# Row places in a GNN kernel: running counts per block in PSUM, and block additions spread over VectorE's step

## What is computed

```python
h = jnp.maximum(_layernorm(x), 0.0)
# layer 0: mean over neighbours, two products, log_softmax
x = x + _L0_gnn_ref(h, edge_index, W_l, W_r, b)
h = jnp.maximum(_layernorm(x), 0.0)
# layer 1
weight = jnp.maximum(edge_rbf @ W1 + b1, 0.0) @ W2 + b2   # edge_rbf: 206250 x 64
hl = h @ Wl + bl
msg = hl[dst] * weight
x = x + segment_sum(msg, src)      # the sum goes by src, the unsorted side
```

## Time and profile before

| | |
|---|---|
| median of 3 runs | 3465.89 us |
| span of the profiled execution | 3469.3 us |
| busy share of the span | PE 86%, weight loads 70%, DVE 79%, ACT 60%, POOL 52% |
| instructions that DVE ran | 7718 |
| chain that ended last, by engine | DVE 36%, PE 32%, issue 17%, DVEq 7%, DMA 4% |

### The profile page before, as it was taken

How to read it: one execution, slowest core, us unless ns; L and a number is a source line. 1 busy time by engine, 2 the same in 40 slices (tenths; PEclk the granted TensorE clock), 3 DMA queues, 4 the chain that set the end, 5 groups by cost and what they waited for, 6 DMA issues and landing times.

```text
span 3469.3 us, 97235 instructions
## 1 busy us (share of the span) xinstructions
PE 2987.6 (86%) x26330; PEld 2437.6 (70%) x26331; DVE 2757.6 (79%) x7718; ACT 2085.3 (60%) x4907; POOL 1808.5 (52%) x1790
## 2 busy tenths in 40 slices
PE   0799999999668878899999989988889898998977
PEld 0699999999655556776766666766667666766766
DVE  8899999999786657777777777777777777777866
ACT  2599999998353335555555545555455555555656
POOL 3400010000127777667766676666766677677750
PEclk9999999999868889999999999999999999999999
DMA  3198888960103336666666656655666666666657
GB/s 117 37 326 313 311 309 310 311 213 3 38 19 107 103 103 172 179 175 160 178 164 161 160 150 172 166 162 147 166 168 180 165 158 184 173 158 175 181 154 207
DMA packets 506188, 593.04 MB, mean 171 GB/s; under 512 B 71050, under 2 KB 477058, under 8 KB 505905
## 3 DMA queue, kind: packets, MB, share of 16 engines
q1 hardware_dynamic: 449506, 470.49, 49.4%
q0 software_dynamic: 56400, 119.07, 9.9%
HBM read 293.94 MB, written 295.35 MB: 170 GB/s over the span
## 4 chain that ended last, share of the span: by engine, by line
DVE 36%; PE 32%; issue 17%; DVEq 7%; DMA 4%; POOL 2%; ACT 1%; SPq 0%; POOLq 0%; ACTq 0%
PE PS L1119 11%; DVE X L1017 8%; PE PS L1110 5%; DVE big L990 4%; PE PS L1282 4%; PE PS L1249 4%; DMA messages<-big,idxr 4%; DVE big L978 3%; DVE aux L768 3%; DVEq L1012 3%; DVE big L964 2%; DVE big L975 2%; DVE big L967 2%; DVE hpar L1006 2%; PE PS L1261 2%
## 5 line engine op out<-in xcount | busy, mean ns | idle before, releaser
L605 POOL DMA_INDIRECT messages<-big,idxr x1664 | 1637.0, 984 | 720.8 <-issue 466.5
L1282 PE MATMUL PS<-big,hpar 128*128 128x128 f32 x5120 | 663.8, 283 | 163.7 <-DVE hpar L1006 128.7
L1282 PEld LDWEIGHTS PS<-big,hpar 128*128 128x128 f32 x5120 | 610.5, 195 | 223.1 <-DVE hpar L1006 181.2
L1432 ACT ACTIVATE big<-PS,b1c 128x512 f32<-128x512 f32 x416 | 286.0, 688 | 708.3 <-PE PS L1238 708.3
L1017 DVE TENSOR_TENSOR X<-X,PS 128x128 f32 x1280 | 368.7, 288 | 325.3 <-PE PS L1282 131.9
L1119 PE MATMUL PS<-h_parts,counts 128*128 128x258 f32 x3626 | 565.3, 296 | 0.0
L1359 ACT ACTIVATE counts<-PS 128x784 fp32r<-128x784 f32 x592 | 481.7, 825 | 93.9 <-PE PS L1110 85.6
L1249 PE MATMUL PS<-W2s,big 128*128 128x128 f32 x3328 | 500.8, 295 | 0.0
L1249 PEld LDWEIGHTS PS<-W2s,big 128*128 128x128 f32 x3328 | 419.0, 197 | 98.3 <-issue 98.3
L1119 PEld LDWEIGHTS PS<-h_parts,counts 128*128 128x128 f32 x3626 | 470.2, 191 | 0.2 <-ACT counts L1359 0.2
L1443 ACT ACTIVATE big<-PS 128x512 f32<-128x512 f32 x416 | 247.6, 595 | 347.2 <-PE PS L1261 339.4
(11 more groups left out here) (222 smaller groups left out, 3639.1 us busy)
## 6 DMA issues: line engine op xcount, KB each, us to landing
messages<-zeros SPq DMA_DIRECT2D x896, 193.5 KB
big<-messages SPq DMA_DIRECT2D x320, 516.0 KB
aux<-slot_rows SPq DMA_DIRECT2D x416, 128.0 KB
big<-in_edge_attr_dram SPq DMA_DIRECT2D x402, 128.0 KB
messages<-big,idxr POOLq DMA_INDIRECT x1664
X<-in_x_dram SPq DMA_DIRECT2D x12, 448.0 KB, 6.9
out_dram<-X SPq DMA_DIRECT2D x6, 448.0 KB
edge_places<-big SPq DMA_DIRECT2D x1, 2496.0 KB, 13.2
```

What stands on the lines that cost most here:

```text
L605: pool.indirect_dma_start(strm_d, bass.IndirectOffsetOnAxis(ap=idxr[:, n % U, j:j + 1], axis=0), outr[:, n % U, j, :], None).then_inc(S_sc ...
L1282: last = nc.tensor.matmul(to[:, r * C:(r + 1) * C], finhot[:, n % 2, r * 2 + q, :], fin[:, k, r, q * ROW:q * ROW + C], start=(q == 0), sto ...
```

## The change

The counts of `taken` move into PSUM. A part's first `ranks` writes the starts of its blocks into `pQ` by a product with the identity, and every later one adds to `pQ` what has passed since: the rows of the step before (in a ring `hotW` of RING = 8 steps) and those of the step's own earlier tiles. `pQ` then holds each place outright. VectorE multiplies it by the one-hot (`own_places`) and sums straight into the integer `idxr` (`row_places`). `hotU`, `hotV`, `taken`, `place_f` and their operations go.

In VectorE's `layer1` the four block additions are no longer at the end: they stand between the other operations of the next step, the load of their places comes before `messages`, and `one_hot_T` moves to the end. Rows that belong to no block get a stretch of the stream for each part, which isn't zeroed; that makes 42 of 896 zeroing transfers fewer.

```diff
-    IR = 6
+    RING = 8
...
-        pQ = PS[:, 6, 0:5 * NBK].rearrange("p (j b) -> p j b", j=5)
+        pQ = PS[:, 6, 0:J * NBK].rearrange("p (j b) -> p j b", j=J)
...
             def block_hot(g, n):
...
-                dve.wait_ge(S["hot_ready"], g * 3 + 1)
-                nc.vector.tensor_tensor(hotU[:, 2:, :], hotW[:, s, 1:, :], hotW[:, s, 0:J, :], ALU.add).then_inc(S["hot_ready"], 1)
-                dve.wait_ge(S["hot_ready"], g * 3 + 2)
-                nc.vector.tensor_tensor(hotV[:, s, 1:, :], hotU[:, 2:, :], hotU[:, 0:J, :], ALU.add).then_inc(S["hot_ready"], 1)
+            def own_places(g, n):
+                at = n % RING * J
+                dve.wait_ge(S["rank_done"], g + 1)
+                wait(dve, S["rank_chain"], g * 2)
+                nc.vector.tensor_tensor(place, pQ, hotW[:, at:at + J, :], ALU.mult).then_inc(S["rank_chain"], 1)
 
             def row_places(g, n):
...
+                k = n % U
+                dve.wait_ge(S["rank_chain"], g * 2 + 1)
                 wait(dve, S_sc[k], (g - k) * 16)
-                nc.vector.tensor_copy(idxr[:, k, :], place_f).then_inc(S["rank_chain"], 1)
+                with nc.allow_low_precision(reason="one term of each sum is not zero"):
+                    nc.vector.tensor_reduce(idxr[:, k, :], place, AX, ALU.add).then_inc(S["rank_chain"], 1)
...
             def layer1(s, n, o):
...
+                add(0)
                 if not isinstance(s, int) or s + 2 < G:
                     block_hot(s + 2, n + 2)
+                add(1)
+                if o:
+                    stream_hot(*o)
+                add(2)
+                if more:
+                    own_places(s + 1, n + 1)
+                add(3)
+                if more:
+                    row_places(s + 1, n + 1)
+                if o:
+                    pair_places(o[0])
+                messages(s, n)
                 if more:
                     one_hot_T(s + 1, n + 1)
-                if o:
-                    stream_hot(*o)
-                messages(s, n)
-                if more:
-                    row_places(s + 1, n + 1)
-                if adding[0]:
-                    block_adds(o[0] - 1 if o else adding[0][0], pFL[adding[0][1] % 2])
                 adding[0] = o
...
             def ranks(g, n):
-                pe.wait_ge(S["hot_ready"], g * 3 + 3)
-                wait(pe, S["rank_chain"], g * 5)
-                nc.tensor.matmul(pQ, onesb[:, :], hotV[:, n % 2, :, :], start=True, stop=False)
-                nc.tensor.matmul(pQ[:, 0:J, :], tri[:, :], hotW[:, n % 2, 1:, :], start=False, stop=True).then_inc(S["rank_done"], 1)
+                at = n % RING * J
+                pe.wait_ge(S["hot_ready"], g + 1)
+                wait(pe, S["rank_chain"], g * 2 - 1)
+                opens = FIRST.index(g) if isinstance(g, int) and g in FIRST else None
+
+                def counted(before, j, t, tiles):
+                    nc.tensor.matmul(pQ[:, j:j + tiles, :], before[:, :], hotW[:, t:t + tiles, :], start=False, stop=False, skip_group_check=True)
...
+                elif at:
+                    counted(upto, 0, at - J, J)
+                    for k in range(1, J):
+                        counted(onesb, 0, at - J + k, J)
+                else:
...
+                        counted(onesb, 0, (RING - 1) * J + k, J - k)
+                        counted(onesb, J - k, 0, k)
+                nc.tensor.matmul(pQ, tri[:, :], hotW[:, at:at + J, :], start=False, stop=True, skip_group_check=True).then_inc(S["rank_done"], 1)
```

More of the change, by code:

```diff
@@ L55, in gnn_program @@
     NOCT = sum(OCTS)
-    CAP = NOCT * FO + P
-    CAP += -CAP % 3
-    assert all(o * FO >= n + 2 * NB for o, n in zip(OCTS, SLOTS)) and (CAP - NOCT * FO) * P >= NS * P - E
+    BIN = -(-(NS * P - E) // P)
+    ZF = NOCT * FO + -NOCT * FO % 3
+    CAP = ZF + NPART * BIN
+    assert all(o * FO >= n + 2 * NB for o, n in zip(OCTS, SLOTS))
     NPAIR = NOCT * FO // 2
@@ L222, in gnn_program @@
         oht = part(big, used, GE).bitcast(bf16).rearrange("p (s f) -> p s f", s=2)
[L223 to L228, removed]
+        hotW = part(big, used, RING * J * NBK // 2).bitcast(bf16).rearrange("p (t b) -> p t b", t=RING * J)
+        place = part(big, used, J * NBK).rearrange("p (j b) -> p j b", j=J)
         away = part(big, used, FO // 2 * P).rearrange("p (t v) -> p t v", t=FO // 2)
@@ L330, in gnn_program @@
         BIAS_OPS = 2 * (3 + 4 + 4)
-        NZ = CAP * ROW // ZW
-        assert NZ * ZW == CAP * ROW
+        NZ = ZF * ROW // ZW
+        assert NZ * ZW == ZF * ROW
         def chunk(c):
@@ L827, in split_starts @@
             def split_starts():
-                nc.vector.tensor_copy(starts[:, 0, NB:], starts[:, NPART - 1, NB:])
+                for p in range(NPART):
+                    last = nc.vector.memset(starts[:, p, NB:], float((ZF + p * BIN) * P))
+                last.then_inc(S["starts_ready"], 1)
                 link(nc.vector.tensor_copy(split, starts[:, 0, 1:NB]))
@@ L949, in _ @@
             dve.wait_ge(S["z_done"], NCH)
[L950 to L953, removed]
             def one_hot_T(g, n):
@@ L995, in _ @@
             block_hot(1, 1)
+            own_places(0, 0)
             row_places(0, 0)
@@ L1009, in stream_hot, with pair_places, block_add @@
                                         ALU.is_equal).then_inc(S["finhot_ready"], 1)
-            def block_adds(i, sums):
-                dve.load(pair_regs, bq_i[0:1, ds(i * (FO // 2), FO // 2)])
-                ats = [dve.snap(pair_regs[r], min_val=0, max_val=(NB - 1) * C) for r in range(FO // 2)]
-                dve.wait_ge(S["finmm_done"], i + 1)
-                for r, at in enumerate(ats):
-                    wait(dve, S["fadd_done"], i * (FO // 2) + r)
-                    nc.vector.tensor_tensor(Xf[:, ds(at, C)], Xf[:, ds(at, C)], sums[:, r * C:(r + 1) * C], ALU.add)\
-                        .then_inc(S["fadd_done"], 1)
+            def pair_places(i):
+                dve.load(pair_regs, bq_i[0:1, ds(i * (FO // 2), FO // 2)])
+            def block_add(i, r, sums):
+                at = dve.snap(pair_regs[r], min_val=0, max_val=(NB - 1) * C)
+                dve.wait_ge(S["finmm_done"], i + 1)
+                wait(dve, S["fadd_done"], i * (FO // 2) + r)
+                nc.vector.tensor_tensor(Xf[:, ds(at, C)], Xf[:, ds(at, C)], sums[:, r * C:(r + 1) * C], ALU.add).then_inc(S["fadd_done"], 1)
+            def block_adds(i, sums):
+                pair_places(i)
+                for r in range(FO // 2):
+                    block_add(i, r, sums)
             adding = [None]
@@ L1045, in _ @@
             steps(dve, layer1, next_part)
-            block_adds(OCT0[-1] - 1, pFL[(OCT0[-1] - 1) % 2])
+            for r in range(FO // 2):
+                block_add(OCT0[-1] - 1, r, pFL[(OCT0[-1] - 1) % 2])
             def segment(i, n):
```

48 lines of the change are left out of this document (25 added, 23 removed).

## The result

The changed kernel takes 3348.76 us (median of 4 runs, 3342.59 to 3351.83), the kernel before 3464.15 us (4 runs in the same series): a ratio of 0.966, interval 0.965 to 0.968. The forecast was 3353 us, with a range of 3286 to 3430. The profiled execution of after has a span of 3349.9 us.

The account below looks back on a forecast made before the run. VectorE (5.90 us) was taken to bound steps with an oct, PE (5.35) afterwards. The stage: 416 x 5.14 = 2138, plus 67 = 2205 us, 113 less; 3469.3 - 113 - 3.4 = 3353 us, range 3286 to 3430.

Parts of the forecast that it names:

- VectorE sets 5.90 us, and 0.70 us of it is the register load: Steps with an oct, before: VectorE sets 5.90 us; its 0.70 us hole before the block additions is the register load.
- What the change takes off VectorE: VectorE's step with an oct: 1.25 us of busy time goes, leaving 4.0 to 5.3 us, some 4.5 in the middle.
- PE 5.06 + 0.29 = 5.35 us: PE's step with an oct: 5.06 us without waits, plus 0.29 for 550 more columns, the new bound at 5.35 us.
- In a step without an oct ... about 3.85 us: PE held at `node_rows` by `messages` and `one_hot_T`: about 3.85 us, below POOL's step, so no cost.
- POOL's lead of 5 us: POOL's issued work ahead at each loop's start: about 5 us, full because the 12 written-out steps average 4.35 us.
- POOL's waits, 67 us: Loops of parts 1 to 6: 6 us each in 1 and 5, 3.5 in 6, 30 in 2 and 3, 22 in 4.
- The lower clock at back edges: 16-step loops: PE stops 4.31 us, then runs at a lower clock, `node_rows` 1.77 us instead of 0.83.
- The 13.2 us of the whole step: PE's step at a 16-step back edge, before: 13.2 us, 8.1 too many; put at 8.4 us with the added columns.
- rival 1: POOL becomes the bound everywhere: 3286 us without the 67 us, 3243 with scatters at their median too; chance 0.13.
- PE's 8-step loops: Rival 2: these loops start to stop at back edges too, about 72 us, 3425 us; chance 0.10.
- The five matmuls: Rival 3, in `ranks`: they don't overlap, 5 x 0.25 us, a step with an oct 6.02 us, 3520 us; chance 0.07.
- The sum: Stage of 416 steps: 2138 + 67 = 2205 us instead of 2318.6, 113 us less, giving 3353 us.

## Why the prediction came out right, and where it didn't

- **VectorE sets 5.90 us, and 0.70 us of it is the register load.** Right, and shown by moving the load alone: the step shown lost 0.47 us and the kernel 101 us.
- **What the change takes off VectorE.** The 1.25 us are right: from the first scatter to the last VectorE is busy for 1222.5 us instead of 1739.2, 1.24 us less for each of 416 steps. Its whole step, forecast at 4.0 to 5.3 us, came to 3.48 us in the step shown (2444.63 to 2448.11). The sum added up whole rows, and VectorE's rows overlap: `one_hot_T` (L955) starts 0.08 us before the end of `messages` (L981). It cost nothing, since PE is the slower one. But the sum treated the 1.25 us as what the gain needs. Either the counting or the load's place is enough: 104 and 101 us alone, 115 us for the whole change, since PE and POOL stand right below VectorE's old step. The new order by itself, which I had as a part of the gain, costs 84 us.
- **PE 5.06 + 0.29 = 5.35 us.** Right: 5.29 us in the step shown. The price of 550 columns (0.24 us) is borne out by the three added matmuls (0.26 us a step for 600).
- **"In a step without an oct ... about 3.85 us. That is below POOL's step, so it costs nothing."** The first sentence held (3.82 us in the step shown), the second failed: `node_rows`, released last by `one_hot_T`, then runs 1.67 us instead of 0.83, which makes the step behind longer. Where such steps follow each other, in part 0, one takes 4.86 us (median). Moving `one_hot_T` gave 17 us back.
- **POOL's lead of 5 us.** 2 to 3 us at the loops' starts, for the same reason: the written-out steps of parts 1 to 6, forecast at 4.35 us, averaged 5.0 to 5.3. After the move POOL was some 6 to 8 us behind `messages` in parts 0 and 1.
- **POOL's waits, 67 us.** 51 us, each wait above 0.45 us less its 0.30 us summed. Part 4's two at back edges are 7.32 and 7.13 us (6.61 before) and the largest; it has 24 us in all, forecast 22. Parts 2 and 3 were put at 15 us each; part 3 has 18, part 2 only 4, where PE's loop is hardly fetched anew.
- **The lower clock at back edges.** I put `node_rows`' 1.77 us down to it. In the kernel before, the granted clock is 0.79 over those matmuls (2593.2 to 2595.1 us) and 0.50 only behind them, and the same 12 take 1.67 us at 1.00 where they are held. So their delay need not be the clock's. The 13.2 us of the whole step were read right, and the sum rests on those.
- **Rivals.** POOL's scatters didn't get shorter (985 ns). The three operations that rival 1 named don't show: the kernels here that keep them have scatters of 977 to 994 ns on average, those without them 985 to 994 ns. But the Trainium skill's rule on two-input VectorE operations, cited there, isn't refuted by this. `stream_hot` (L998) reads two tiles of SBUF and stays, and in after the scatters that run beside it for over 0.1 us take 1093 ns on average, those that don't touch it 960 ns. As the block additions and `own_places` often run beside the same scatters, no run separates them. PE's 8-step loops didn't stop in after. The five matmuls overlap (0.09 us apart), so nothing got slower.
- **The sum.** Stage 2198 us against 2205 forecast. Part 2 is 11 us below its share (395 us against 406, with few stops) and part 0 4 us below; parts 3 and 4 are 3 to 4 us above. In part 5 luck helped: the 6 us of waits didn't come, but its scatters took 1013 ns instead of 984, 6 us in 52 steps. The time was hit closer than its terms were.

## What to carry to other kernels

Before taking work off the bounding engine, look for the stretch in which it runs nothing: here a register load that left VectorE idle for 0.70 us a step was worth as much as a new way of counting that took 1.25 us of work off it. Once VectorE no longer set the step, hiding the same load gave nothing that is clear of noise. In an order written out by hand, ask of each engine's last operation who waits for it, and of its first what it waits for: where both are the same partner, the two engines' steps make one loop. And of an experiment that only lengthens or shortens a loop, read the transfers of instructions in the loops behind it before believing its time.

## What was not expected of the hardware

- 12 matmuls with 12 weight loads take 0.83 us where PE arrives late, and 1.67 to 1.69 us where it has been held for their operand, at a granted clock of 1.00 both times. The rows show no operation between them; that the register work of each can't be done ahead is my explanation, and was not tried.
- Whether a loop is fetched anew at its back edge goes by more than its length. Loops of the same 16 steps had 12 and 38 transfers in parts 2 and 3 of after, and with PE's program of before it is the other way round (38 and 19). In the one pair compared it is worth some 15 us a part. The Trainium skill (the section named above) says that a branch back stalls when its target has left the instruction window; the stops agree, and by the runs the place in the program matters as well as the length.
